# TensorE's order in an attention slot: the scores ahead of the transposes of the probabilities

## The reference

```
x = x + layernorm(attention(layernorm(x)))     # 16 heads of 64, keys and values through a rank of 128
x = x + layernorm(experts(layernorm(x)))       # each token goes to one of 8 experts, 128 -> 512 -> 128

att = softmax(where(causal, q k^T / 8, -inf));  y = att v;  out = y w_out
```

## Time and profile before

| | |
|---|---|
| median of three runs | 1287.67 us |
| profiled execution | 1290.58 us, span from first to last instruction 1286.4 us |
| TensorE matmuls, weight loads | busy 95% and 86% of the span |
| VectorE, ScalarE, GpSimd | busy 88%, 83%, 72% |
| granted TensorE clock, mean | 0.978 |
| chain that ended last | 86% of it on TensorE |

### The profile page before, as it was taken

The page is one execution under the profiler, slowest core; times in us unless marked ns, Lnnn a source line. Parts: engine busy times, 40 slices in busy tenths (PEclk is TensorE's granted clock), DMA queues, the critical chain, the costliest instruction groups (busy, mean ns, idle before and its releaser), DMA issues.

```text
span 1286.4 us, 42145 instructions
## 1 busy us (share of the span) xinstructions
PE 1221.9 (95%) x12784; PEld 1105.4 (86%) x12785; DVE 1130.4 (88%) x4457; ACT 1062.5 (83%) x3244; POOL 924.2 (72%) x1495
## 2 busy tenths in 40 slices
PE   7999999999999999999999999999999997599992
PEld 6888888888888888888888888888888886599982
DVE  5999999999999999999999999999999995488873
ACT  4999898999999999999999999999999893466661
POOL 4577777777777777777777777777777665067775
PEclk8999999999999999999999999999999997799997
DMA  5000000000000000000000000000000003333320
GB/s 228 6 10 18 16 16 16 16 16 16 16 16 16 16 16 16 16 16 16 16 16 16 16 16 16 13 16 14 15 16 13 15 15 123 98 97 101 96 84 13
DMA packets 39233, 43.03 MB, mean 33 GB/s; under 512 B 4802, under 2 KB 35398, under 8 KB 38800
## 3 DMA queue, kind: packets, MB, share of 16 engines
q1 hardware_dynamic: 33536, 29.43, 7.6%
q0 software_dynamic: 5648, 13.00, 2.7%
HBM read 25.16 MB, written 18.16 MB: 34 GB/s over the span
## 4 chain that ended last, share of the span: by engine, by line
PE 86%; issue 5%; POOL 3%; DVE 1%; ACT 1%; SPq 1%; DMA 1%; POOLq 0%; ACTq 0%; DVEq 0%
PE psZU L682 17%; PE psS L605 14%; PE psZU L697 14%; PE psP L649 10%; PE psZU L685 7%; PE psT L619 5%; PE psT L620 5%; PE psT L621 5%; PE psS L292 3%; POOL out L456 2%; PE psZU L306 2%; PE psT L306 1%; PE psP L584 1%; PE psM L736 1%; PE psM L727 1%
## 5 line engine op out<-in xcount | busy, mean ns | idle before, releaser
L1219 POOL TENSOR_TENSOR softmax<-softmax,rinv 128x256 f32<-128x256 f32 (+1 forms) x512 | 413.2, 828 | 213.8 <-DVE rinv L947 213.0
L781 ACT ACTIVATE softmax<-softmax,nmax 128x128 f32<-128x128 f32 (+1 forms) x1024 | 453.8, 451 | 9.1 <-DVE nmax L923 8.3
L923 DVE CUSTOM_DVE_ANT_0 softmax<-psS,mask 128x128 f32<-128x128 f32 (+1 forms) x1024 | 321.6, 352 | 5.6 <-PE psS L605 1.1
L932 DVE TENSOR_TENSOR p_both<-psP,p_both 128x768 fp32r<-128x768 f32 x256 | 243.8, 952 | 0.9 <-ACT p_both L745 0.9
L745 ACT ACTIVATE t_hi<-psT 128x512 fp32r<-128x512 f32 x256 | 153.0, 598 | 84.0 <-PE psT L621 78.0
L911 DVE TENSOR_TENSOR t_lo<-psT,t_hi 128x512 fp32r<-128x512 f32 x256 | 175.3, 685 | 41.9 <-ACT t_hi L745 40.8
L745 ACT ACTIVATE p_both<-psP 128x768 fp32r<-128x768 f32 x256 | 206.6, 807 | 2.3 <-PE psP L649 2.3
L781 ACT ACTIVATION_READ_ACCUMULATOR softmax<-softmax,nmax 128x1 f32 x1024 | 199.1, 194 | 0.0
L952 DVE TENSOR_TENSOR z_lo<-psZU,z_hi 128x512 fp32r<-128x512 f32 x256 | 175.3, 685 | 20.0 <-ACT z_hi L745 18.1
L605 PE MATMUL psS<-t_hi,t_lo 64*128 64x128 f32 (+1 forms) x1024 | 164.5, 317 | 0.4 <-DVE nmax L923 0.4
L682 PE MATMUL psZU<-p_both,xk_hi 128*128 128x512 f32 x512 | 160.7, 395 | 0.0
(11 more groups left out here) (197 smaller groups left out, 3192.0 us busy)
## 6 DMA issues: line engine op xcount, KB each, us to landing
softmax<-routed_rows SPq DMA_DIRECT2D x39, 260.0 KB, 2.7
routed_rows<-padr SPq DMA_DIRECT2D x8, 520.0 KB, 4.9
wx<-ffn_w SPq DMA_DIRECT2D x2, 2058.0 KB, 13.0
xin<-x SPq DMA_DIRECT2D x32, 128.0 KB, 2.2
xres<-x SPq DMA_DIRECT2D x32, 128.0 KB, 2.1
out<-wq_s,ids POOLq DMA_INDIRECT x78
wup_s<-wup SPq DMA_DIRECT2D x1, 1024.0 KB, 5.9
routed_rows<-pay,dst POOLq DMA_INDIRECT x64
```

The costliest lines, as they stand in the source:

```text
L781: last = nc.scalar.activation(prob[:, pb, h, a:z], nscore[:, (s - lag) % 2, h, a:z], ACT.Exp, bias=nmax[:, pb, h, q:q + 1], scale=-1.0, ac ...
L923: last = v.tensor_tensor_reduce(nscore[:, n1, h, a:z], psS[:, h, a:z], mask[:, a:z], -1.0, -MASKED, ALU.add, ALU.min, nmax[:, p1, h, q:q + 1])
L932: v.tensor_tensor(by_half(p_lo, s % 2), psPh, by_half(p_hi, s % 2).bitcast(F32), ALU.subtract).then_inc(S["p_split"], 1)
L1219: last = g.tensor_tensor(pr, pr, rinv[:, p2, :, q:q + 1].broadcast_to([P, 2, z - a]), ALU.mult)
```

## The change

S, with its two waits, is issued in front of PT with its waits and the small transposes that go with it. Behind PT now comes the ranking of `r == 6` and then Z. The set-up matmuls of the first four slots move along with S; PT does not run in those.

```diff
--- before.py
+++ after.py
@@ -622,6 +622,17 @@
                     last.then_inc(S["t_ready"], 1)
                 if s == B_SLOTS and not live(s + 1):
                     pe.wait_ge(S["b_split"], HD // P)
+                if setup_slot(s, live):
+                    if s == 0:
+                        values()
+                    head_matrices(2 * s)
+                    head_matrices(2 * s + 1)
+                if live(1):
+
+                    pe.wait_ge(S["t_split"], g0 + s)
+                    if live(2):
+                        pe.wait_ge(S["nmax_ready"], 2 * (g0 + s - 1))
+                    scores((s - 1) % 2)
                 if live(4):
 
                     freed = g0 + s - 4
@@ -650,17 +661,6 @@
                                                        prob[half, s % 4, h, k * P:(k + 1) * P], ident[half, half])
                             if n == 5:
                                 last.then_inc(S["pt_ready"], 1)
-                if setup_slot(s, live):
-                    if s == 0:
-                        values()
-                    head_matrices(2 * s)
-                    head_matrices(2 * s + 1)
-                if live(1):
-
-                    pe.wait_ge(S["t_split"], g0 + s)
-                    if live(2):
-                        pe.wait_ge(S["nmax_ready"], 2 * (g0 + s - 1))
-                    scores((s - 1) % 2)
                 if r == 6 and live_b(2):
 
                     pe.wait_ge(S["onehot_ready"], b0 + db - 1)
```

## The result

The kernel with the changed order takes 1358.65 us (median of four runs, 1357.46 to 1360.32). The kernel before, run on the same chip, takes 1288.76 us (1287.29 to 1291.41). The ratio is 1.0538, with a 95% interval of 1.0519 to 1.0558: 69.9 us slower, where 48 were forecast. The profiled execution took 1360.32 us.

The account below looks back on a forecast made before the run. TensorE was taken as the bound, busy 1013 of 1014 us; each slot becomes the longer of its work and the loop through m1. Excesses of 1.56 us a block over 31 blocks give 48 us: 1336 us, range 1306 to 1370.

Parts of the forecast that it names:

- The signs named for it: TensorE idle at S (0.1 us plain, 0.8 behind slot 2), ScalarE idle before p_hi, VectorE waiting for p_hi.
- two unknown steps: Last pair of S to first transposes, taken as 0.12 us (0.03 to 0.21); last transposes to p_hi, 0.37 (0.22 to 0.49).
- The loop of slot 2: S, PT, p_hi, p_lo, m1, next S, with extra transposes and copies in slot 2: 4.87 us against 4.05.
- the release of S: 0.15: Wait from the end of m1's last read-out to S of the next slot, read early in the kernel: 0.15 us.
- The plain loop: S, PT, p_hi, p_lo, m1, next S in a plain slot: 4.01 us against TensorE's 3.92 to 3.94.
- The second chain: p_hi, four exponentials, z_hi, z_lo, t_lo, m0, next p_lo: 4.81 us, just hidden under the 4.85 left to it.
- Slot 5's loop into slot 6: Routing steps on VectorE in slot 5 lengthen the loop through m1 to 4.30 us against 3.93, excess 0.37.
- In slot 6 (4.41 on TensorE) the same kind of steps stays hidden.: VectorE's routing steps in slot 6 add nothing to TensorE's slot: excess 0.
- Only slot 2 stalls: Rival: plain loop 3.77 us stays inside 3.92; slot 2 costs 0.58 and slot 5 about 0.17; 1311 us, chance 0.14.
- The clock: Rival: stalls halve TensorE's clock for a 3.3 us stretch in each block, some 51 us more: 1387 us, chance 0.05.
- Faster: Rival: TensorE's shape change from PT to Z becomes free, saving 0.09 us in 252 slots: 1265 us, chance 0.05.
- no difference: Rival: slack on VectorE and ScalarE (63 and 95 us) swallows the change: 1288 us, chance 0.04.

Follow-up runs that it names:

- g2_four: Changed kernel with the sum as a reduction, m1 ahead of p_lo, z_hi between the exponentials, and misc_late (normalising) behind z_lo: 1292.29 us.
- e3_max: Changed kernel with VectorE's second maximum, m1, and the routing step behind it ahead of p_lo in every slot: 1343.51 us, ratio 1.0416.
- g1_mend: Changed kernel with the sum as a reduction, z_hi between the exponentials, and the old order in slots with r = 2: 1304.83 us.
- e1_add: Changed kernel with the addition of 1 on VectorE replaced by a reduction over two columns: 1339.15 us, ratio 1.0375.
- e2_r2: Changed kernel with the old order (PT ahead of S) in slots with r = 2 alone: 1339.01 us, ratio 1.0381.
- e7_add_r2: Changed kernel with the sum as a reduction and the old order in slots with r = 2: 1319.67 us, ratio 1.0222.
- f2_zhi: Changed kernel with ScalarE's z_hi between the two pairs of exponentials: 1327.45 us, ratio 1.0277.

## Why the prediction was right, and where its size was off

- **Direction, place and mechanism of the first stall: right.** S waits for the maxima, behind slot 2 most of all; undoing the order there alone gives back 21 us. The signs named for it are there: ScalarE waits for PT ahead of p_hi (92.3 us in 187 slots) and VectorE for p_hi (30.0 us in 89). The 0.1 us at S in plain slots is not.
- **The total, 69.9 us against 48, fell in the range partly by luck.** The range's upper part stood for the high ends of two unknown steps, and those came out near the values taken. What filled it is a cost that the sum had at nothing, in slot 6.
- **The loop of slot 2: 4.75, forecast 4.87.** The term that was too large is "the release of S: 0.15". Here it is 0.05 (544.74 to 544.79); what else the row held that it was read from, early in the pipeline, no run shows. The two steps that no row showed were taken well: last pair of S to the transposes 0.12 (540.72 to 540.84), and last transposes to p_hi 0.29 to 0.37 in plain slots.
- **The plain loop: forecast 4.01, about 3.91 by the trace after,** 0.10 of it the same release. In slots 0 and 1 the last read-out ends at most 4.66 after T; with 0.05 for the release, S of the next slot could start at 4.71, or 3.91 behind its own. So S does not wait in plain slots: it starts 0.80 after T in slots 0 to 2, as PT did before. The 0.06 and 0.05 more in slots 0 and 1 come from Z, which starts 0.14 behind the end of z_lo; with z_lo early (g2_four) both slots take 3.91. The forecast of 0.08 and 0.09 was near by luck.
- **The second chain was not "just hidden".** The 0.04 us were the distance to a loop of 4.01. With TensorE's own 3.93 in its place the chain's 4.81 is longer than 3.93 + 0.84, by 0.04. And "Z's other waits (p_lo and z_lo of the slot before) are met before S's, as m1 stands behind p_lo" holds for p_lo alone: z_lo stands behind m1 on VectorE. Z waits for it in slots 0 and 1, and for 0.55 us in slot 3 as soon as S does not (e3_max).
- **Slot 5's loop into slot 6: right.** S of slot 6 waits 0.26 to 0.35, forecast 0.37. In the full change this lies inside the 1.26 of slot 6, whose end L736 sets.
- **The step that failed: "In slot 6 (4.41 on TensorE) the same kind of steps stays hidden."** TensorE stands about 0.9 us a block at L736, 28 us over 31 blocks; less those, the change would cost 42 us. The prediction had "TensorE never waits there", but L736 already followed the end of dsel by 0.05 us before the change. Slot 6 grows by what L736 is later: by 0.15 us in g2_four (L736 0.15 later), 0.46 in g1_mend (0.45), 0.57 in e1_add (0.59) and 1.26 in the full change (1.23). In the full change 0.69 of that is L1033 (5.59 less 4.90 in e1_add): the late z_lo moves it into GpSimd's second piece, where it takes 0.77 us; the working took durations of rows as fixed and did not ask what runs beside a moved instruction.
- **The rivals.** Only slot 2 stalls: half right, for the plain slots' S do not, but slots 4 and 6 do. The clock: false, 1.00 from 36 to 1110 us, where TensorE was busy for 95% of the time. Faster and no difference: false; with nearly every wait mended the order is still not faster, 1.0024 (1.0012 to 1.0037).
- **Left open:** in e2_r2 and e7_add_r2 slot 3 keeps 4.12, 0.19 over its old length, with S still waiting there; the chain behind that was not taken apart.

## What to carry to other kernels

When work on an engine that sets the pace is moved, write down every loop that passes through it and a buffer that exists once, and add the slot's length to each: a loop hidden by 0.04 us is not hidden. A list of waits can miss one that a modelled end covers: look for starts that follow another engine's end at a fixed distance, since such a place has no slack. A cost that one edit removes can return at once through the next loop of the same length, so test edits together as well as one by one. An instruction that moves on a second engine may also land beside other work on a third, and its duration is then not the one in the old profile.

## What the hardware showed that was not expected

An addition on 128 x 2 numbers in SBUF got longer with the time that a piece of GpSimd's multiplication still had to run when it began: 0.16 us with 0.12 to run (the kernel before), 0.20 with 0.19 to run (f2_zhi), and 0.77 in the median, up to 0.92, with 0.75 in the median to run (the kernel after). In all 29 long cases it ended 0.02 to 0.03 us after the piece. A reduction that makes the same sums took 0.15 us in the same place, where in 29 of 32 cases 0.73 to 0.90 of the piece were still to run (e1_add). The Trainium skill (SBUF — State Buffer, Who interferes with whom) says that VectorE and GpSimd share one pair of ports as an exclusive lock: a scalar operation in a two-port mode that comes second waits for GpSimd's whole instruction, and a reduction on this chip never contends. The trace agrees with both, with the numbers above; that the addition ran in a two-port mode no run shows.
